# Channel mixing by 32x32 products, router logits by column groups, weight parts on VectorE, expert loads moved

## What is computed

```
att   = softmax(gelu(gelu(cond @ W0 + b0) @ W1 + b1) @ W2 + b2)      # 64 x 8
agg_w = einsum('bk,koi->boi', att, weight)                           # a 32x32 matrix per batch
xt    = einsum('boi,bih->boh', agg_w, x) + (att @ bias_k)[:, :, None]
logits = xt @ router_w + router_b                                    # 2048 x 16
scores = softmax(logits) + router_bias                               # 4 groups of 4, best 2 groups, best 2 experts
y = sum over chosen e of score_e * (silu(xt @ w1_e + b1_e) * (xt @ w2_e + b2_e)) @ w3_e + b3_e
z = (silu(xt @ sw1 + sb1) * (xt @ sw2 + sb2)) @ sw3 + sb3            # shared expert
out = x + y + z
```

## Time and profile before

| | us |
|---|---|
| median of three runs | 253.44 (252.91 to 253.76) |
| the profiled execution | 253.9 |
| its span | 252.1 |
| TensorE busy | 241.7 (96%) |
| VectorE, ScalarE, GpSimd busy | 127.8, 78.4, 109.7 |
| first mixing product | 15.18 |
| first shared product | 53.35 |
| first product of the expert loop | 97.09 |

### The profile page before, as it was taken

One profiled execution on the slowest core, in us unless ns is written; L12 is line 12 of the kernel. 1 busy time (PEld: TensorE's weight loads), 2 busy tenths in 40 slices (PEclk: granted clock), 3 DMA queues, 4 the chain that ended last, 5 costly groups with the idle time before them and its releaser, 6 DMA issues.

```text
span 252.1 us, 4013 instructions
## 1 busy us (share of the span) xinstructions
PE 241.7 (96%) x1147; PEld 164.6 (65%) x1148; DVE 127.8 (51%) x268; ACT 78.4 (31%) x169; POOL 109.7 (44%) x128
## 2 busy tenths in 40 slices
PE   7969999999999889999999999999999999999993
PEld 7927777788875446767777777777777754444441
DVE  0193332269879887333333333333333311198995
ACT  3214555413149000333333333333333321110210
POOL 7196566410030355466666666666664331000080
PEclk9968999999999999999999999999999999999999
DMA  6999979887508938954555455455554222999974
GB/s 195 322 405 387 314 226 371 295 274 294 213 37 313 420 100 259 361 174 155 170 165 170 139 153 161 135 166 166 166 166 166 84 91 49 364 388 388 395 292 166
DMA packets 20843, 58.37 MB, mean 231 GB/s; under 512 B 2549, under 2 KB 2677, under 8 KB 20572
## 3 DMA queue, kind: packets, MB, share of 16 engines
q1 hardware_dynamic: 15228, 40.35, 44.6%
q0 software_dynamic: 5600, 17.83, 21.6%
HBM read 41.39 MB, written 17.30 MB: 233 GB/s over the span
## 4 chain that ended last, share of the span: by engine, by line
PE 87%; DVE 9%; issue 2%; DVEq 0%; ACT 0%; POOL 0%; POOLq 0%
PE psum L536 76%; PE psum L688 6%; PE psum L586 3%; DVE xT L1161 2%; PE psum L701 2%; DVE xT L910 1%; DVE xt_sb L1161 1%; DVE x_early L910 1%; DVE r L935 1%; DVE xt_sb L910 1%; DVE r L1117 0%; DVE code_f L1095 0%; DVE late_region L910 0%; ACT late_region L806 0%; DVE mix_bias L931 0%
## 5 line engine op out<-in xcount | busy, mean ns | idle before, releaser
L536 PE MATMUL psum<-wexp,r 128*128 x272 | 68.4, 381 | 0.5 <-DVE r L1117 0.4
L536 PEld LDWEIGHTS psum<-wexp,r 128*128 128x128 f32 x272 | 48.5, 190 | 22.9 <-issue 16.9
L477 POOL DMA_INDIRECT expert_rows<-late_region,to_row x33 | 33.3, 1010 | 33.5 <-ACT late_region L853 33.5
L910 DVE TENSOR_TENSOR r<-psum,ebias 128x256 f32<-128x256 f32 x34 | 14.4, 425 | 64.7 <-PE psum L536 64.7
L471 POOL DMA_INDIRECT late_region<-xt_rows,from_row x36 | 35.3, 982 | 17.1 <-issue 10.5
L536 PE MATMUL psum<-wexp,xt_sb 128*128 x68 | 34.8, 594 | 0.0
L536 PE MATMUL psum<-xT,shared_sb 128*128 128x512 f32 x64 | 28.0, 593 | 0.1
L847 ACT ACTIVATE r<-r 128x128 f32<-128x128 f32 x34 | 10.5, 309 | 55.4 <-DVE r L910 55.4
L853 ACT ACTIVATE late_region<-psum 128x512 f32<-128x512 f32 x34 | 20.3, 598 | 15.8 <-PE psum L536 15.8
L1117 DVE COPY r<-psum 128x512 f32<-128x512 f32 x36 | 24.5, 680 | 0.0
L688 PE MATMUL psum<-ident,late_region 128*128 128x128 f32 x144 | 21.6, 273 | 0.9 <-DMA late_region<-xt_rows,from_row 0.9
(11 more groups left out here) (173 smaller groups left out, 291.8 us busy)
## 6 DMA issues: line engine op xcount, KB each, us to landing
wexp<-expert_pack SPq DMA_DIRECT2D x16, 768.0 KB, 6.1
wexp<-expert_rows SPq DMA_DIRECT2D x8, 1024.0 KB, 12.8
xt_rows<-xt_sb SPq DMA_DIRECT2D x16, 256.0 KB, 3.8
x_early<-x SPq DMA_DIRECT2D x2, 1024.0 KB, 10.1
late_region<-x SPq DMA_DIRECT2D x2, 1024.0 KB, 15.0
ebias<-expert_bias SPq DMA_DIRECT2D x1, 2048.0 KB, 7.8
out_dram<-x_early SPq DMA_DIRECT2D x8, 256.0 KB, 9.6
shared_sb<-shared_pack SPq DMA_DIRECT2D x1, 1536.0 KB, 18.6
```

What stands on the lines that cost most here:

```text
L477: nc.gpsimd.indirect_dma_start(out=y_dram[:, :], out_offset=bass.IndirectOffsetOnAxis(ap=rows_of.bitcast(U32), axis=0), in_=y_sb[:, slot, ...
L536: return nc.tensor.matmul(dst, lhsT, rhs, start=start, stop=stop)
L910: return nc.vector.tensor_tensor(dst, a, b, op)
```

## The change

- x is loaded per group by four DMAs into 32 partitions each, instead of one into 128. Partition 32 r + i of position q then holds channel i of batch 4 r + q of the group, so that one position holds one batch of each of the group's four tiles.
- Mixing: per group sixteen products of a 32x32 matrix by 512 columns. Product (q, r) reads partitions 32 r and on (row group r) and writes partitions 32 q and on (column group q) of bank r, which is tile r of the group. `mixT` holds only the 32x32 matrices; `r1` is no longer zeroed. The transposes use banks 5 and 6.
- The start: ScalarE copies the biases and one row group of four of the matrices (`mix_copied_too`); VectorE the other three. The first transposes wait for all of these copies.
- Router: per group four products with 32 columns of `router_w` (16 of them zero) as the stationary operand and 512 tokens moving, each chunk of columns of x into its own column group of bank 7 (`chunk_logits`); VectorE copies that bank (L979), and per tile one product with `chunk_sum` (16 columns, ones where the row's place in its column group equals the expert) adds the four chunks (`logits`). Both come a group late in the loop; the last group's stand between shared products.
- The four coarse parts of the shared weights go from ScalarE to VectorE (L993); GpSimd takes them in between those of x, and the first shared block waits for eight of the twelve.
- SyncE starts an expert load after each fourth tile instead of each second; the other four follow the loop, and then the first two groups of x are loaded again in natural order, which `shared_sum` waits for.
- The scratch for descriptors of GpSimd's DMAs is 8192 bytes instead of the default 16384.

The core of the diff:

```diff
@@ SyncE
-                sp.dma_start(dst, group_of_x(g)).then_inc(x_loaded[g], 16)
+                for r in range(BPT):
+                    first = (g * BPT + r) * BPT
+                    sp.dma_start(dst[r * IN_C:(r + 1) * IN_C], x[first:first + BPT].rearrange("q i d -> i q d")
+                                 ).then_inc(x_loaded[g], 16)
...
-                if t % 2 == 1:
-                    place = HALF + t // 2
+                if t % GT == GT - 1:
+                    place = HALF + t // GT
                     sp.dma_start(wexp[:, place, :], expert_pack[place]).then_inc(half_loaded[0], 16)
+            for place in range(HALF + NG, E):
+                sp.dma_start(wexp[:, place, :], expert_pack[place]).then_inc(half_loaded[0], 16)
+            for g in range(EARLY):
+                sp.dma_start(x_early[:, g * GT:(g + 1) * GT, :], group_of_x(g)).then_inc(x_natural_loaded, 16)
@@ GpSimd
-            link(nc.gpsimd.memset(att_rows, 0.0))
-            nc.gpsimd.memset(r1[:, :], 0.0).then_inc(blocks_zeroed, 1)
+            nc.gpsimd.memset(att_rows, 0.0).then_inc(blocks_zeroed, 1)
...
-            for u in range(SPLITS):
-                pool.wait_ge(part_ready, u + 1)
+            W = EARLY * GT
+            for u in (0, 1, W, 2, W + 1, 3, W + 2, W + 3, *range(GT, W)):
+                pool.wait_ge(*((part_ready, u + 1) if u < W else (w_part_ready, u - W + 1)))
@@ TensorE
+            def chunk_logits(g):
+                if g == 0:
+                    pe.wait_ge(router_loaded, 16)
+                pe.wait_ge(xT_ready, (g + 1) * GT)
+                for c in range(C):
+                    last = mm(psum[c * EC:(c + 1) * EC, 7, :], rw_sb[:, c, :], xT[:, g, c, :])
+                last.then_inc(chunk_logits_done, 1)
+
+            def logits(g):
+                if g == 0:
+                    pe.wait_ge(chunk_sum_ready, 1)
+                pe.wait_ge(chunk_logits_ready, g + 1)
+                for t in range(g * GT, (g + 1) * GT):
+                    last = mm(psum[:, 4, t * E:(t + 1) * E],
+                              logits_by_chunk[:, g % 2, (t % GT) * P:(t % GT + 1) * P], chunk_sum[:, :])
+                last.then_inc(logits_done, 1)
+
+            for s in range(NT):
+                if s % GT == 0:
+                    g = s // GT
+                    pe.wait_ge(x_loaded[g], 16 * BPT)
+                    pe.wait_ge(mix_copied, g + 1)
+                    pe.wait_ge(mix_copied_too, g + 1)
+                    if g > 0:
+                        pe.wait_ge(xt_ready, s)
+                    for q in range(BPT):
+                        for r in range(BPT):
+                            rows = slice(r * IN_C, (r + 1) * IN_C)
+                            last = mm(psum[q * IN_C:(q + 1) * IN_C, r, :], mixT[rows, g, q, :],
+                                      x_tile(s + q)[rows, :])
+                    last.then_inc(xt_done, GT)
+                if s % GT == 1 and s > GT:
+                    chunk_logits(s // GT - 1)
+                if s % GT == GT - 1 and s > GT:
+                    logits(s // GT - 1)
+                pe.wait_ge(xt_ready, s + 1)
+                if s == 0:
+                    pe.wait_ge(mix_copied, NG)
+                    pe.wait_ge(mix_copied_too, NG)
...
-            pe.wait_ge(split_ready, SPLITS)
-            shared_up(0, 0)
-            shared_up(0, 1)
+            pe.wait_ge(split_ready, SPLITS - GT)
+            shared_up(0, 0, between={(0, 0): lambda: chunk_logits(NG - 1), (0, 1): lambda: logits(NG - 1)})
+            shared_up(0, 1)
+            pe.wait_ge(split_ready, SPLITS)
             shared_up(1, 0)
@@ ScalarE
+            act.wait_ge(pe_cond, 5)
+            for r in range(BPT):
+                rows = slice(r * IN_C, (r + 1) * IN_C)
+                nc.scalar.activation(mix_bias[rows, :], mixes_bias[rows, r], ACT.Copy).then_inc(bias_copied, 1)
+            for g in range(NG):
+                copy_mixes(lambda dst, src: nc.scalar.activation(dst, src, ACT.Copy), g, BPT - 1
+                           ).then_inc(mix_copied_too, 1)
...
-                if 2 <= t < 2 + SPLITS:
+                if 2 <= t < 2 + EARLY * GT:
@@ VectorE
+            def copy_chunk_logits(g):
+                dve.wait_ge(chunk_logits_done, g + 1)
+                if g >= 2:
+                    dve.wait_ge(logits_done, g - 1)
+                V.tensor_copy(logits_by_chunk[:, g % 2, :], psum[:, 7, :]).then_inc(chunk_logits_ready, 1)
...
+                if t % 2 == 1 and 1 < t < GT * 2 + 2:
+                    if t == 3:
+                        dve.wait_ge(shared_loaded, 16)
+                    whole, part, _ = split_of(EARLY * GT + t // 2 - 1)
+                    V.tensor_copy(part, whole).then_inc(w_part_ready, 1)
+            copy_chunk_logits(NG - 1)
@@ program
-    nc = bacc.Bacc("TRN2", target_bir_lowering=False, num_devices=1)
+    nc = bacc.Bacc("TRN2", target_bir_lowering=False, num_devices=1, dynamic_dma_scratch_size=8192)
```

100 lines of the change are left out of this document (42 added, 58 removed).

## The result

| | before | after |
|---|---|---|
| median, us | 253.50 (252.48 to 253.76, 6 runs) | 256.12 (254.99 to 257.06, 6 runs) |
| ratio of the times | | 1.0106, 95% interval 1.0074 to 1.0139 |
| profiled execution, us (span) | 253.9 (252.1) | 257.06 (255.3) |
| first mixing starts | 15.18 | 12.92 |
| first weight part | 39.65, no wait for the weights | 31.79, as they land |

A forecast was written before the change was run, and what follows sets the result against it. TensorE was taken to bound stage one at 2.19 us a tile; groups of 6.5 us instead of 8.76, after start and store waits, gain 7.6 us: 245.8 us, range 243.0 to 255.0 (the forecast's own 243.0 to 248.5, chance 0.36).

The forecast's parts named there:

- The start: Bias and mix copies shared with ScalarE: mixing can start at 13.9 us, not 15.18; first transposes wait until 17.3.
- Mixing and chunk logits: TensorE in stage one, per group: sixteen 32x32 products take 1.15 us, the four 32-column router products 0.95 us.
- Rivals 2 and 3: Column groups don't overlap: mixing 3.5 us, 264.3 us, chance 0.12; they half overlap: mixing 2.1 us, 254.3 us, chance 0.10.
- The group chain: Steady part of stage one: 6.5 us per group of four tiles against 8.76, set by ScalarE, not TensorE.
- The stores and the weights: Tile 4's eviction needs tile 0's store, queued behind the shared weights: weights at 24.5 us, eviction at 25.2.
- Rival 1: Loads of x into 32 partitions run at half rate: 6.7 us of gain lost, 250 to 255 us, chance 0.28.
- The clock: TensorE at 1.2 GHz after the pause at the start: first two mixings 2.3 us each, first transposes 0.9.
- Rival 4: TensorE's clock stays at 1.2 GHz: 250.5 us if until 35 us, 260.5 if through stage one; chance 0.08.
- What is moved behind: GpSimd's weight parts, four expert loads and the second load of x follow later, all covered, at no cost.
- the scratch: Halved descriptor scratch of GpSimd's queue: priced at nothing, named among the rest, which had chance 0.06.
- The sum: Shared products start at 43.1 us, comparable point 45.8 against 53.35: gain 7.6 us, 245.8 us against the median.

## Why the prediction was wrong, step by step

- **The start.** Right in its mechanism: mixing begins 1.2 us after the first copy (forecast 1.15). That it came at 12.92 and not 13.9 is luck of one execution, whose copies began at 11.68 and not at 12.76; the runs of this form have 12.7 to 14.1.
- **Mixing and chunk logits.** Right: 1.14 and 1.07 us at full clock (forecast 1.15 and 0.95); column groups overlap. Rivals 2 and 3 are out.
- **The group chain.** Right with whole loads: 6.12 us (forecast 6.5).
- **The stores and the weights: this step failed.** "I put its eviction at 25.2 us (weights at 24.5 ...)" took the loads of x at the old rate with a little for the issues of twelve more. They ran at little more than half (200 to 224 GB/s against 322 to 405). Weights 31.8, eviction 32.5. With whole loads: 22.9 and 23.7.
- **Rival 1's price.** Mechanism and times right to 0.6 us, the price too low. It gave 250 to 255 and a chance of 0.28. The 6.7 us that it took off stage one were really 8.9 (31.8 against 22.9), since in the forecast itself the weights came too late, and it gave 2.5 us for a clock that cost 4.1 (from 42.7 where I had let it recover within a group). That the times fit so well is in part luck. By its own terms, 15.7 - 7.9 us on top of 24.5, the weights land at 32.3, not 31.5, and the ratio in the sentence behind it gives 30.3, not 31. One reading under it was wrong as well: the loads of x did not run at the highest rate of the trace (405 GB/s, where slice 14 of the earlier trace rows has 420), though near it, so that there was little slack. That should have raised the chance, since nothing but the equal size of the pieces spoke against it.
- **The clock.** Rival 4 stood as one of its own, at 0.08. It came as the consequence of rival 1: in the stall of 10.7 us the clock fell (at 25.7), and it came back at 42.7. The two were not alternatives, and their prices add.
- **What is moved behind.** Right but for the scratch: loads, second load of x and weight parts stayed covered, the first expert product follows the first shared one by 46.05 us, where before had 43.74; the difference of 2.3 is the router work of the last group that now lies between (forecast 2.7). The scratch, a term that the sum had put at nothing, cost 0.8 to 1.2.
- **The sum.** With whole loads the comparable point is 40.5 + 2.3 = 42.8, against 45.8 forecast and 53.35 before: the gain in stage one was 3 us larger than forecast (tile 4's eviction 1.5 us sooner, the three groups behind it 1.1 shorter, the router work 0.4 less), and 1 us went with the scratch. The profiled execution of that kernel, the fastest of its four, was 9.1 us under that of before, with a granted clock of 0.986; the other three have 0.970 to 0.976, and the medians are 7.3 apart (forecast 7.6). So 246.0 beside 245.8 is in part luck: a gain in stage one that was forecast 3 us too small stands against the scratch and a clock that was low for longer in most executions. Term by term the forecast was right to 1.5 us but for the loads' rate.

## To carry to other kernels

A transfer that fills only one half of the partitions runs at little more than half the rate here (190 to 230 GB/s, for 32 and for 64 partitions alike), and a layout that makes TensorE's products smaller has to be charged for it wherever the loads have no slack: some 7 us of gain were paid for with 10 us of loads and clock. Before costing what a faster engine saves, write down what stands behind each transfer on its queue and when it lands; a stall also costs the clock behind it (of 10.7 us here, and still one of 4.8 us in the run with two queues). Where moving a transfer in the queue seems to cure the wait, ask whether its bytes still have to pass first: all three such moves here only passed the wait on. And the 32x32 products were not needed for the gain: the logits by column groups bring over 4 us, and 128x128 mixing with whole loads is as fast as any kernel here that computes the right result.

## What the runs showed of the hardware

- Rates in slices 2 to 4 of the pages. Whole loads of x: 322 to 405 GB/s before. Pieces of 32 partitions from one queue: 200 to 224 in the changed kernel, 193 to 222 in the one before; halves of 64: 195 to 229; pieces in the order 0, 64, 32, 96: 210 to 252; from two queues: 269 to 298. The lower rate therefore looks like that of the way into one half of the partitions, not that of a queue, and all DMA engines are at work (busy share 1.06 to 1.09 from 7 to 22 us); no run measures that way by itself.
- Loads and stores of 128 partitions whose DRAM side is four blocks: 102 to 104 GB/s, with a busy share of the DMA engines of 0.26 to 0.27.
- Sixteen fp32 products of 32x32 by 512 at full clock: 1.14 us spread over rows and columns, 3.64 on the diagonal, and 3.60 for four 128x128 products.
- With 8192 bytes of descriptor scratch the 57th indirect transfer of 128 rows waits 2.0 us.
- TensorE's clock: at the lower level from 25.7 to 42.7 us after the engine stood from 22.5, at the full one from the fifth slice on when 11 wide idle products filled that stall; at the lower level also from 28.8 to 31.0 behind a stand of 4.8 us (two queues), and at 0.54 from 208.9 to 212.6 behind one of 3.1 us (36 narrow products).
